# A delta-rule tail and an RWKV-style last stage: operands kept in PSUM, filler matmuls, table loads moved, token blend moved from activations into weights

## The reference, cut to what matters

```
h = layernorm(x)                       # 4 x 512 rows, T = 512, 16 heads of 8
q, k = l2norm(h Wq)/sqrt(8), l2norm(h Wk);  v, gate = h Wv, h Wg
beta = sigmoid(h Wb);  decay = -exp(A_log) softplus(h Wa + dt_bias)
within chunks of 64 tokens: (I + P + ...) v, running sums of decay
over chunks: S_new = S exp(g) + k^T v_new;  o = q exp(g) S + attn v_new
x = x + (rmsnorm(o) * norm_w * silu(gate)) Wo

h = layernorm(x);  h_prev = h one token earlier (0 ahead of the first)
xr = mu_r h + (1 - mu_r) h_prev;   xk = mu_k h + (1 - mu_k) h_prev
x = x + sigmoid(xr Wr^T) * (relu(xk Wk^T)^2 Wv^T)
```

## Time and profile before

| | us |
|---|---|
| median of 3 runs | 977.53 |
| lowest, highest | 977.09, 977.79 |
| the profiled execution | 973.23 |
| its span, first to last instruction | 970.7 |
| busy PE, weight loads, DVE, ACT, POOL | 683.4, 486.3, 654.1, 387.8, 229.3 |

### The profile page before, as it was taken

The page is one execution under the profiler, slowest core; times in us unless marked ns, Lnnn a source line. Parts: engine busy times, 40 slices in busy tenths (PEclk is TensorE's granted clock), DMA queues, the critical chain, the costliest instruction groups (busy, mean ns, idle before and its releaser), DMA issues.

```text
span 970.7 us, 21668 instructions
## 1 busy us (share of the span) xinstructions
PE 683.4 (70%) x9090; PEld 486.3 (50%) x9090; DVE 654.1 (67%) x1259; ACT 387.8 (40%) x920; POOL 229.3 (24%) x216
## 2 busy tenths in 40 slices
PE   3899999899999999999998779987300000000586
PEld 2677777567766667666666645555200000000574
DVE  6367776256666566665552773255999999999766
ACT  2655656433232333233303311128565455444034
POOL 6300000100000000000002000310777878787410
PEclk9999999999999999999979779998755555555567
DMA  4100000000000000000000004000000000000001
GB/s 178 22 5 12 13 14 7 7 2 1 5 11 2 1 13 2 2 2 2 2 2 2 2 0 88 1 1 2 1 0 0 0 1 0 0 0 0 1 1 44
DMA packets 8065, 10.97 MB, mean 11 GB/s; under 512 B 1296, under 2 KB 5648, under 8 KB 7840
## 3 DMA queue, kind: packets, MB, share of 16 engines
q1 hardware_dynamic: 7968, 9.60, 3.8%
HBM read 6.41 MB, written 1.08 MB: 8 GB/s over the span
## 4 chain that ended last, share of the span: by engine, by line
PE 56%; DVE 22%; issue 13%; POOL 4%; ACT 4%; DMA 0%; DVEq 0%; SPq 0%; POOLq 0%; ACTq 0%
PE PS L564 8%; PE PS L540 7%; PE PS L439 5%; PE PS L345 4%; PE PS L357 4%; PE PS L333 3%; PE PS L556 3%; PE PS L526 3%; PE PS L687 2%; DVE arena L620 2%; PE PS L325 2%; PE PS L446 2%; PE PS L700 2%; DVE arena L1237 1%; DVE arena L1245 1%
## 5 line engine op out<-in xcount | busy, mean ns | idle before, releaser
L620 DVE TENSOR_TENSOR arena<-PS,C 128x512 f32<-128x512 f32 x160 | 105.6, 686 | 100.7 <-PE PS L540 100.6
L900 PE MATMUL PS<-arena 64*64 64x8 f32 x112 | 8.4, 256 | 196.6 <-DVE arena L1289 192.7
L1013 ACT ACTIVATE arena<-arena 128x128 f32<-128x128 f32 x256 | 81.8, 390 | 95.9 <-DVE arena L1245 95.9
L900 PEld LDWEIGHTS PS<-arena 64*64 64x64 f32 x112 | 7.1, 213 | 199.4 <-DVE arena L1257 194.2
L540 PE MATMUL PS<-arena 64*64 64x512 f32 x640 | 89.7, 631 | 7.9 <-DVE arena L620 7.9
L564 PE MATMUL PS<-arena 128*64 128x18 f32 x2560 | 88.7, 211 | 0.0
L564 PEld LDWEIGHTS PS<-arena 128*64 128x64 f32 x2560 | 85.4, 141 | 0.5
L1102 POOL TENSOR_TENSOR arena<-arena 128x1024 f32<-128x1024 f32 x32 | 75.1, 2348 | 41.2 <-DVE arena L1245 41.2
L1518 POOL TENSOR_TENSOR arena<-arena 128x512 f32<-128x512 f32 x4 | 5.0, 1268 | 337.7 <-PE PS L564 337.7
L470 ACT ACTIVATE arena<-PS 128x512 f32<-128x512 f32 (+1 forms) x48 | 23.5, 524 | 137.8 <-PE PS L441 85.5
L389 DVE TENSOR_REDUCE arena<-PS 128x4 f32<-128x512 f32 x64 | 43.9, 686 | 30.5 <-PE PS L333 30.5
(11 more groups left out here) (253 smaller groups left out, 1517.2 us busy)
## 6 DMA issues: line engine op xcount, KB each, us to landing
W<-wpack SPq DMA_DIRECT2D x1, 2532.5 KB, 10.6
arena<-arena SPq DMA_DIRECT2D x128, 16.0 KB
arena<-carry_in SPq DMA_DIRECT2D x4, 512.0 KB, 7.9
X<-x SPq DMA_DIRECT2D x4, 256.0 KB, 3.7
out<-X SPq DMA_DIRECT2D x4, 256.0 KB, 2.3
C<-cpack SPq DMA_DIRECT2D x1, 529.0 KB, 6.3
wk<-wkT SPq DMA_DIRECT2D x1, 64.0 KB, 10.5
wv<-wvT SPq DMA_DIRECT2D x1, 64.0 KB, 11.2
```

The source lines that it names most:

```text
L620: e.tensor_tensor(AT[n % 4].rearrange("p (h t) -> p h t", h=8), PS[:, n % 2, :].rearrange("p (h t) -> p h t", h=8), tri.to_broadcast([P, 8 ...
L1013: e.activation(Ra[:, cols], Rs[(t - 1) % 4][:, cols], ACT.Copy, scale=alp[:, t, h:h + 1]).then_inc(l_Ra, 1)
```

## The change

Entry: the four gate products take contiguous columns; the projections use all eight banks, four per quarter, and stay there: no copy to SBUF. DVE makes normalised k and q and beta times v from PSUM (`queries`); `g_used` lets PE write those four banks again. The transposes of the gate rows read every 64th float of banks 4 to 7, so they need all four products. PE writes banks 4 to 7 only after them. ACT's gate functions are no longer placed between the projections of a quarter. Tail: `mask8` and the decay of the last position are copied to bank 6 and read there; 36 filler matmuls (`keep_warm`, bf16, 256 columns) after step 62, two after each carry; `outputs(0)` goes between carries 13 and 14; `states` in another order; the Sqrt and Sigmoid tables are loaded by a dummy activation beforehand. Last stage: POOL multiplies the columns of Wr and Wk by mu and 1 - mu at the start of the delta stage (`Wmix`), `own` and `shift` go, and PE adds two products, one with h and one with h one token earlier, into the same bank.

Ten matmuls stand where five stood; the place behind all `ln_turn` is the same. The core of the diff:

```diff
+        mask8P, egP = PS[:, 6, 64:64 + DH], PS[:, 6, 80:80 + LH]
...
-        xr, xk = take(NB * T), take(NB * T)
+        Wmix = [[wv5[:, (2 * i + k) * P:(2 * i + k + 1) * P] for k in range(2)] for i in range(2)]
...
+        def col(c, o):
...
+            b = 4 * (c % 2)
+            return PS[:, b:b + 4, :].rearrange("p b (t c) -> p (b t) c", t=4)[:, :, o:o + LD]\
+                .rearrange("p t (h d) -> p t h d", h=LH)
...
-                e.matmul(PS[:, 4 + c, :], Wba.rearrange("p j c -> p (j c)"), tokt[:, quarter(c), :], start=True, stop=True)\
+                e.matmul(PS[:, 4 + c, :], Wba.rearrange("p j c -> p (j c)"), hpack[:, c * SEG:(c + 1) * SEG], start=True, stop=True)\
...
-                    e.wait_ge(g_pr, i - 3)
-                    e.wait_ge(g_sq, i - 3)
...
+                if i == 4:
+                    e.wait_ge(g_gd, NQ)
+                if c >= 2 and k == 0:
+                    e.wait_ge(g_used, c - 1)
...
-                        m = e.matmul(PS[32 * j:32 * j + 32, i % 4, s * QW:(s + 1) * QW], tok[:, :, t],
+                        m = e.matmul(PS[32 * j:32 * j + 32, 4 * (c % 2) + k, s * P:s * P + QW], tok[:, :, 4 * i + s],
...
-            e.wait_ge(g_gd, NQ)
...
+                if q == 3:            e.wait_ge(g_gd, NQ)
...
+                keep_warm(e, 5, 2)
...
-                e.wait_ge(t_Sb, q + 1)
+                e.wait_ge(t_Sb, (1, 3, 2, 4)[q])
...
+            e.wait_ge(g_silu, NQ)
+            e.wait_ge(l_R, CH)
+            keep_warm(e, 5, 36)
             for k in range(1, NC1 - 1):
                 carry(k)
-            outputs(0)
+                if k == NC1 - 3:
+                    outputs(0)
...
-                e.activation(pr[:, 4 * i:4 * i + 4, :], t4, ACT.Copy).then_inc(g_pr, 1)
-                if i == 1:
...
-                    e.activation(beta, gd[:, :, 0:LH], ACT.Sigmoid).then_inc(gate_act, 1)
...
-                if i == 3:
...
-                    e.activation(da, da, ACT.Ln).then_inc(gate_act, 1)
-                if i == 5:
...
-                    e.activation(alp, dec, ACT.Exp).then_inc(gate_act, 1)
...
-                    e.activation(eg, gc, ACT.Exp).then_inc(gate_act, 1)
-                if i in (7, 9, 12):
...
+            e.activation(beta, gd[:, :, 0:LH], ACT.Sigmoid).then_inc(gate_act, 1)
...
+            squares(0)
+            root(0)
...
+            e.activation(da, da, ACT.Ln).then_inc(gate_act, 1)
+            squares(1)
...
+            e.activation(alp, dec, ACT.Exp).then_inc(gate_act, 1)
...
+            e.activation(eg, gc, ACT.Exp).then_inc(gate_act, 1)
+            root(1)
+            squares(2)
+            root(2)
+            squares(3)
...
+                    e.activation(mask8P, mask8, ACT.Copy).then_inc(g_mP, 1)
+                    e.activation(egP, eg[:, CH - 1, :], ACT.Copy).then_inc(g_mP, 1)
...
+            e.activation(nwt[:, 0:1], hot8[:, 0:1], ACT.Sqrt)
...
-                    own(e, q - 1)
+            e.activation(nwt[:, 1:2], hot8[:, 0:1], ACT.Sigmoid)
...
-            own(e, NQ - 1)
...
+            for i, mu in enumerate(("mur", "muk")):
+                e.tensor_scalar(omu[:, i:i + 1], w(mu), -1.0, 1.0, ALU.mult, ALU.add).then_inc(h_omu, 1)
...
+            for i, (mu, wt) in enumerate((("mur", "WrT"), ("muk", "WkT2"))):
+                e.tensor_scalar(Wmix[i][0], w(wt), w(mu), None, ALU.mult).then_inc(h_W, 1)
+                e.tensor_scalar(Wmix[i][1], w(wt), omu[:, i:i + 1], None, ALU.mult).then_inc(h_W, 1)
...
-                e.tensor_tensor(h4(kn)[:, quarter(c)], col(pr, LD)[:, quarter(c)], per_head(rs[:, quarter(c), 4:8], n=DH, t=CH // NQ),
...
-                e.wait_ge(g_pr, quarter_in(c))
...
+                e.tensor_tensor(h4(kn)[:, quarter(c)], col(c, LD), per_head(rs[:, quarter(c), 4:8], t=CH // NQ), ALU.mult)\
+                 .then_inc(g_kn, 1)
+                e.tensor_tensor(h4(qn)[:, quarter(c)], col(c, 0), per_head(rs[:, quarter(c), 0:4], t=CH // NQ), ALU.mult)\
+                 .then_inc(g_qn, 1)
...
+                e.tensor_tensor(bb[:, quarter(c), :, 0:DH], col(c, 2 * LD), per_head(beta[:, quarter(c), :], t=CH // NQ), ALU.mult)\
+                 .then_inc(g_used, 1)
...
+            e.wait_ge(g_d, NQ)
+            rows_ = PS[:, 4:8, :].rearrange("p b (n t) -> p t (b n)", t=CH)
...
-                e.wait_ge(g_d, c + 1)
-                e.transpose(gd[:, quarter(c), :].rearrange("p t c -> p (t c)"), PS[:, 4 + c, :]).then_inc(g_gd, 1)
+                e.transpose(gd[:, quarter(c), :], rows_[:, quarter(c), :]).then_inc(g_gd, 1)
...
+            norms(1)
...
-            norms(1)
-            queries(0)
-            values(0)
+            queries(1)
...
-            queries(1)
-            values(1)
...
+            norms(3)
...
-            norms(3)
-            values(2)
...
-            values(3)
...
-                                bc(mask8.rearrange("p (o h x) -> p o h x", o=1, x=1), [P, 8, 8, DH]), ALU.mult).then_inc(t_bd, 1)
+                                bc(mask8P.rearrange("p (o h x) -> p o h x", o=1, x=1), [P, 8, 8, DH]), ALU.mult).then_inc(t_bd, 1)
...
-                elif k == 9:
-                    states(0)
+                elif k in (9, 12):
+                    states(0 if k == 9 else 2)
             states(1)
-            states(2)
-            states(3)
...
+            states(3)
...
-            shift(e, 0)
...
-            shift(e, 1)
...
-            shift(e, 2)
-            shift(e, 3)
...
-                    e.wait_ge(h_mix, 2 * q + 2)
+                    e.wait_ge(ln_hT, 12 + q + 1)
...
+                        e.wait_ge(h_W, 4)
...
-                    e.matmul(PS[:, q % 2, :], w("WkT2"), xk[:, q * SEG:(q + 1) * SEG], start=True, stop=True).then_inc(h_k, 1)
...
+                    past = hT[:, b, PAD + o - 1:PAD + o - 1 + SEG]
+                    e.matmul(PS[:, q % 2, :], Wmix[1][0], hslice(q), start=True, stop=False)
+                    e.matmul(PS[:, q % 2, :], Wmix[1][1], past, start=False, stop=True).then_inc(h_k, 1)
...
-                        m = e.matmul(PS[:, 2 + q % 2, i * P:(i + 1) * P], xr[:, a:a + P], w("WrT"), start=True, stop=True,
...
+                        e.matmul(PS[:, 2 + q % 2, cols], hslice(q)[:, cols], Wmix[0][0], start=True, stop=False,
+                                 skip_group_check=True)
+                        m = e.matmul(PS[:, 2 + q % 2, cols], past[:, cols], Wmix[0][1], start=False, stop=True,
                                      skip_group_check=True)
```

More of the change, by code:

```diff
@@ L224, in program @@
         f_cb = [sem(f"f_cb{tb}") for tb in range(2, NQ)]
-        g_p, g_pr, g_sq, g_ss, g_eps, g_root, g_rec, g_kn, g_qn, g_ready = (
-            sem("g_" + n) for n in ("p", "pr", "sq", "ss", "eps", "root", "rec", "kn", "qn", "ready"))
-        g_ones, g_kba, g_bbv, g_bbk = (sem("g_" + n) for n in ("ones", "kba", "bbv", "bbk"))
+        g_p, g_used, g_sq, g_ss, g_eps, g_root, g_rec, g_kn, g_qn, g_ready = (
+            sem("g_" + n) for n in ("p", "used", "sq", "ss", "eps", "root", "rec", "kn", "qn", "ready"))
+        g_ones, g_kba, g_bbk = (sem("g_" + n) for n in ("ones", "kba", "bbk"))
         gate_act, gate_dve = sem("gate_act"), sem("gate_dve")
@@ L240, in program @@
         h_pad = sem("h_pad")
-        h_omu, h_own, h_mix, h_k, h_r, h_rl, h_ka, h_sr, h_v, h_rv, h_x = (
-            sem("h_" + n) for n in ("omu", "own", "mix", "k", "r", "rl", "ka", "sr", "v", "rv", "x"))
+        h_omu, h_W, h_k, h_r, h_rl, h_ka, h_sr, h_v, h_rv, h_x = (
+            sem("h_" + n) for n in ("omu", "W", "k", "r", "rl", "ka", "sr", "v", "rv", "x"))
         block = ctx.enter_context(nc.Block())
@@ new lines, in squares @@
+            def squares(c):
+                for k in range(4):
+                    i = 4 * c + k
+                    e.wait_ge(g_p, i + 1)
+                    e.activation(Zs[:, 4 * i:4 * i + 4, :], PS[:, 4 * (c % 2) + k, :].rearrange("p (t c) -> p t c", t=4)[:, :, 0:2 * LD],
+                                 ACT.Square).then_inc(g_sq, 1)
+            e.wait_ge(g_gd, NQ)
+            e.activation(beta, gd[:, :, 0:LH], ACT.Sigmoid).then_inc(gate_act, 1)
+            e.wait_ge(gate_dve, V_DZ)
@@ new lines, in delta_act @@
+            e.activation(da, dz, ACT.Abs).then_inc(gate_act, 1)
+            e.activation(eA, w("Alog"), ACT.Exp).then_inc(gate_act, 1)
+            e.wait_ge(gate_act, A_ABS)
+            e.activation(da, da, ACT.Exp, scale=-1.0).then_inc(gate_act, 1)
+            squares(0)
+            root(0)
+            e.wait_ge(gate_dve, V_EX1)
+            e.activation(da, da, ACT.Ln).then_inc(gate_act, 1)
+            squares(1)
+            e.wait_ge(gate_dve, V_DEC)
+            e.activation(alp, dec, ACT.Exp).then_inc(gate_act, 1)
@@ L1018, in gates @@
                 e.wait_ge(g_gate, q + 1)
-                e.activation(gt[:, cols], PS[:, 5 + q % 3, :], ACT.Silu).then_inc(g_silu, 1)
+                e.activation(gt[:, cols], PS[:, 5 + q % 2, :], ACT.Silu).then_inc(g_silu, 1)
             def weigh(q):
@@ L1192, in delta_dve @@
```

(6 more changed lines are left out.)

70 lines of the change are left out of this document (19 added, 51 removed).

## The result

The changed kernel takes 971.78 us (median of 14 runs, 967.6 to 975.88) against 977.97 for the kernel before in the same sessions: ratio 0.9939, 95% interval 0.9918 to 0.9960, or 6.0 us less (3.9 to 8.0). The prediction said 975.6, 969.5 to 982.0.

What follows compares the result with a forecast made beforehand. No engine bounded the entry, DVE the steps and last layernorm and blend, PE's matmuls and clock the end. Terms -6.0 + 0.2 - 0.3 + 4.2 = -1.9 gave 971.3 for the profiled execution, 975.6 as median; range 969.5 to 982.0.

Steps and rivals of the forecast that it cites:

- the second rival: Tail: the fillers keep PE at full clock, so four later groups of matmuls run faster; -3.6, time 972.0, chance 0.14.
- a carry longer than 1.0: Tail: one of the signs listed as showing the prediction wrong; carries were expected to keep their pace of about 0.88 us.
- Entry, -6.0: Delta stage's entry: first step at 694.3 instead of 700.3 us, from faster gate products and a shorter chain, with part-time holds.
- The chain without holds: Entry: the longest chain of operations from gate rows to first step, over four quarters, put at 27.4 us.
- The holds: Entry: three further projection bursts hold up DVE and ACT; 13.5 us if throughout, a third taken, 4.6.
- the third rival: Entry: the bursts meet full clock and each holds DVE and ACT for 4.5 us; entry costs 2.9, time 984.5, chance 0.10.
- the range's lower end of the entry: Entry: with DVE and ACT not held at all, first step at 685.2 us, a gain of 15.1.
- The rule that PE, ACT and DVE's own ports never wait on anyone: Entry, first rival: DVE and ACT are not held, so the entry gives 15.1 us; time 966.5, chance 0.08.
- POOL's scaling, +0.2: Start of the delta stage: POOL's six weight scalings might slow a small DVE operation in the third layernorm; cost 0.2 us.
- Tail, -0.3: Tail: first carry 2.3 us earlier, moving `outputs(0)` costs 1.3, half clock 0.7, fillers 0; net gain 0.3.
- the fourth rival: Tail: fillers delay 14 carries by 0.24 us each and squares run at half clock; +4.2, time 980.1, chance 0.12.
- Last stage, +4.2: Last stage: PE's added products cost 7.0 us, its last turn ends 2.8 earlier; half clock stays 5 us, else 1.7.

Runs made afterwards that it cites:

- token_order: The change with hT stored token position by token position by ACT, so the projections read 32 neighbouring floats: 961.53 us, ratio 0.9831 to the kernel before.
- no_carry_fillers: The change without the two filler matmuls behind each carry, the 36 ahead of them kept: 971.01 us, ratio 0.9944 to the kernel before.
- no_fillers: The change without any filler matmul in the tail, neither the 36 nor the two behind each carry: 971.58 us, ratio 0.9942 to the kernel before.
- outputs_late: The change with `outputs(0)` behind the last carry again, the rest as in the change: 971.79 us, ratio 0.9940 to the kernel before.

## Why the prediction was right

The time lies inside the range, and inside the forecast's own (971.5 to 979.5) at its low end. The sum had a gain of 1.9; measured are 6.0 by the ratio and 7.9 in the traces, so it was 4 to 6 us too cautious. The time is also that of the second rival, 972.0, but its mechanism did not come (see the tail). And one of the prediction's own signs of being wrong did: a carry longer than 1.0. Term by term, traces against the working:

- **Entry, -6.0: -9.0 in the traces, -7.4 (5.5 to 9.4) alone.** Gate rows were put 10.8 us after the first gate product and came after 9.4: only the first two transposes were held, and the stride of their reads, put at up to 1.3, cost nothing (0.67 with PE silent). The chain without holds was put at 27.4 and is 24.8, as token_order shows it (656.46 to the first step at 681.25): the products of 0.69 follow each other at 0.60, and the later small operations take 0.23 to 0.29. The holds were put at 4.6 and took 5.6 (39.82 - 9.37 - 24.8). That this came so near is in part the luck of the clock. The prediction had the bursts that follow a wait at half clock, because 2 us without work had gone ahead of half clock in the kernel before. The third burst was at half clock, but the fourth began at full clock after 2.05 us without work. In no_carry_fillers the clock stayed full through 3.74 us without work between the same two bursts. There and in no_fillers the same entry took 43.4 and 43.0, with holds of about 9: the third rival in part. What failed here besides is the cause. The holds come from the stride of the operand, which the text did not have, so they were no price of the number of small matmuls, and the range's lower end of the entry could be had by moving data.
- **The rule that PE, ACT and DVE's own ports never wait on anyone** ("SBUF — State Buffer", section "SBUF: two separate sides", in the Trainium skill) fell as the rows said: 3.00 and 3.88 stand beside the strided operand. The same page of the Trainium skill has what the prediction did not use, in its section "Door 1: The DMA port swizzle": each access that crosses to a new 16-byte line pays, so floats can be read at a stride of up to four of them for free. The gate products agree as far as they go, 7.0 us at a stride of 64 floats and 3.7 without; no run here has a stride of two to four. That other engines are held by it is in these traces alone.
- **POOL's scaling, +0.2:** nothing (5.30 and 5.29 us, above). The steps took 0.3 more in every kernel with the new entry; the cause is open.
- **Tail, -0.3: -1.6** (42.73 to 41.13 from the last step to the first turn). The first carry came 1.9 earlier for the 2.3, with 0.47 given back in the copy of 16 columns. The fillers, put at 0 because DVE would answer in that time, cost 1.7 in nine carries of 1.07, and 2.1 by no_fillers: the mechanism of the fourth rival, at half to two thirds of its bound of 3.4. Moving `outputs(0)` was put at 1.3 of cost, though the three terms named there add up to 1.55, and is 0.5 (20.49 against 20.02 in outputs_late). The stretch after them was put 0.7 longer and was 2.4 shorter, by the clock. So the tail came out near its -0.3 by luck: the fillers' price and the clock cancel, and the clock's part is that of one execution. The second rival, full clock through the carries, did not come: 0.50 at 905 to 914. Without any filler (no_fillers) the stretch after the squares is as short, 15.97.
- **Last stage, +4.2: +2.4** in the traces. Turn and scaling came 2.65 earlier for 2.8, and a quarter is 1.76 longer, as worked out; but half clock lasted about 1 us into the queue, not 5, so the price fell to near the lower end of 1.7. The same queue took 18.2 to 19.8 in the kernels that have it, so the price is 2.4 to 3.9 with the clock.

So the direction of each stage and the added products on PE held. Wrong were the cause of the holds, the fillers' price of nothing, the chain of the entry (2.6 too long) and where half clock falls.

## What to carry to other kernels

Before a stage is reordered round an engine that is held up, ask what holds it: here a re-laid operand, written by a copy that was there anyway, took 12.0 us off the entry, the reordering 9.0. Work moved from one engine to another should stop where it leaves the critical path: one quarter of the blend belongs on PE, the others beside it. And a move into idle time is judged by what stands behind it in that engine's list.

## What the runs showed of the hardware

A stationary operand of 32 floats that lie 256 bytes apart, at full PE clock, holds DVE and ACT nearly for as long as PE reads (a transpose takes 3.90 instead of 0.67, an addition 3.00 instead of 0.43, a Sigmoid 3.88 instead of 0.42), even where they touch only SBUF; with neighbouring floats the addition takes 0.43 and the Sigmoid 0.42 at the same clock, 1.00. At half clock little is held: a sum takes 1.30 instead of 1.21. And where PE's clock falls differs from run to run in code that is the same: a stretch of unchanged work ran at a mean of 0.90 in one execution and 0.85 in another, and the tail's stretch from squares to turn, with the same instructions, took between 16.2 and 20.7 us.
